# Moving the first weight loads of a fused attention and feed-forward kernel to ScalarE's queue, and a load and its statistics behind the spills and packs

## The reference

```python
x = x + layernorm(attn(layernorm(x)))   # 16 heads of 32, rotary positions,
                                        # each token sees itself and the 128 before it
x = x + layernorm(ffn(layernorm(x)))

def ternary_quant(w):
    scale = mean(abs(w)) + 1e-8
    return clip(round(w / scale), -1, 1) * scale

def ffn(x):                             # W_up, W_gate: 2048 x 512, W_down: 512 x 2048
    up, gate = x @ ternary_quant(W_up).T, x @ ternary_quant(W_gate).T
    return (silu(up) * gate) @ ternary_quant(W_down).T
```

## Time and profile before

| what | value |
|---|---|
| median of 3 runs | 1320.64 us (1318.81 to 1321.5) |
| the profiled execution | 1321.27 us, its span 1319.1 us |
| granted TensorE clock, mean | 0.994 |
| TensorE busy | 1289.1 us (98% of the span) |
| VectorE busy | 938.5 us (71%) |
| ScalarE busy | 794.9 us (60%) |
| GpSimd busy | 709.1 us (54%) |
| DMA | 178.17 MB, mean 135 GB/s |

### The profile page before, as it was taken

The page is one execution under the profiler, slowest core; times in us unless marked ns, Lnnn a source line. Parts: engine busy times, 40 slices in busy tenths (PEclk is TensorE's granted clock), DMA queues, the critical chain, the costliest instruction groups (busy, mean ns, idle before and its releaser), DMA issues.

```text
span 1319.1 us, 28382 instructions
## 1 busy us (share of the span) xinstructions
PE 1289.1 (98%) x9972; PEld 909.3 (69%) x9972; DVE 938.5 (71%) x2421; ACT 794.9 (60%) x1468; POOL 709.1 (54%) x959
## 2 busy tenths in 40 slices
PE   8889999999999999999999999999999999999997
PEld 6566766767677766767677676777667677666775
DVE  7777888776788767876778777787678767634333
ACT  3798887666465665656665665656656556533332
POOL 3365778645655546645565465555566353425432
PEclk9899999999999999999999999999999999999999
DMA  7865657757677577775688576876767746610000
GB/s 233 257 183 161 179 144 145 162 111 155 137 156 162 117 157 150 165 143 120 131 164 171 120 151 134 160 161 120 153 118 170 144 87 123 126 33 25 25 17 33
DMA packets 392797, 178.17 MB, mean 135 GB/s; under 512 B 318416, under 2 KB 372048, under 8 KB 392656
## 3 DMA queue, kind: packets, MB, share of 16 engines
q1 hardware_dynamic: 391792, 174.79, 60.5%
q10 hardware_dynamic: 864, 1.57, 0.4%
HBM read 71.89 MB, written 25.17 MB: 74 GB/s over the span
## 4 chain that ended last, share of the span: by engine, by line
PE 90%; DVE 3%; DMA 2%; ACT 2%; issue 1%; POOL 0%; SPq 0%; ACTq 0%; POOLq 0%; DVEq 0%
PE J L1613 29%; PE Y L1631 16%; PE J L1550 14%; PE J L1541 8%; PE J L1560 8%; PE S L1613 5%; PE O L1525 4%; PE S L1493 3%; PE Y L1501 1%; DMA W<-in_w_qkv 1%; DMA Qp<-spill 1%; DMA spill<-split 1%; PE S L1489 1%; PE S L1490 1%; DVE room L1324 0%
## 5 line engine op out<-in xcount | busy, mean ns | idle before, releaser
L1631 PE MATMUL Y<-down_q,room 128*128 128x512 fp8e4 x1024 | 262.3, 379 | 0.6 <-DVE room L1340 0.6
L1550 PE MATMUL J<-xnT,W 128*128 128x512 f32 x512 | 242.7, 600 | 2.5 <-ACT xnT L977 2.4
L1018 ACT ACTIVATE prob<-prob,peak 128x256 f32<-128x256 f32 x512 | 229.7, 498 | 16.9 <-DVE peak L1270 16.7
L1270 DVE CUSTOM_DVE_ANT_0 prob<-S,band,neg_score_scale 128x256 f32<-128x256 f32 x512 | 225.7, 478 | 10.4 <-PE S L1490 5.4
L1613 PE MATMUL J<-xT,gate_q 128*128 128x256 f16 x1760 | 210.2, 273 | 4.1 <-DVE room L1324 4.1
L1613 PE MATMUL J<-xT,up_q 128*128 128x256 f16 x1776 | 212.0, 273 | 0.0
L1074 ACT ACTIVATE room<-J,sig_scale 128x512 f32<-128x512 f32 x111 | 76.2, 687 | 215.1 <-PE J L1613 215.1
L1613 PEld LDWEIGHTS J<-xT,gate_q 128*128 128x128 fp8e4 x1760 | 171.3, 98 | 49.5 <-DVE room L1324 8.7
L1613 PEld LDWEIGHTS J<-xT,up_q 128*128 128x128 fp8e4 x1776 | 173.4, 98 | 43.8 <-DVE room L1334 1.6
L1324 DVE SCALAR_TENSOR_TENSOR room<-room,J 128x512 f32<-128x512 f32 x111 | 76.3, 687 | 173.8 <-ACT room L1074 173.8
L868 POOL TENSOR_TENSOR o_n<-o_raw,rinv 128x128 f32<-128x128 f32 x128 | 53.9, 421 | 270.3 <-DVE rinv L1299 270.0
(11 more groups left out here) (171 smaller groups left out, 2020.6 us busy)
## 6 DMA issues: line engine op xcount, KB each, us to landing
spill<-split SPq DMA_DIRECT2D x64, 256.0 KB, 2.5
Qp<-spill SPq DMA_DIRECT2D x127, 128.0 KB, 2.9
Kp<-spill SPq DMA_DIRECT2D x125, 128.0 KB, 2.9
x_in<-in_x SPq DMA_DIRECT2D x32, 256.0 KB, 3.2
X<-in_x SPq DMA_DIRECT2D x32, 256.0 KB, 3.4
out_x<-X SPq DMA_DIRECT2D x32, 256.0 KB, 3.2
Kc<-Kp SPq DMA_DIRECT2D x32, 128.0 KB, 3.0
turned<-parts SPq DMA_TRANSPOSE x198, 3.2
```

Of the source, the lines that this page charges most:

```text
L1018: e = nc.scalar.activation(prob[:, prob_home(U), a, :], prob[:, prob_home(U), a, :], ACT.Exp, bias=peak[:, prob_home(U), a:a + 1], scale=-1.0)
L1270: e = nc.vector.tensor_tensor_reduce(out=prob[:, prob_home(U), a, :], in0=S_ps[U % 2][:, a * 2 * P:(a + 1) * 2 * P], in1=mask[:], scale=ne ...
L1550: e = pe.matmul(dst[:], W[:, part, c, g * P:(g + 1) * P], xnT[:, c, :], start=(c == 0), stop=(c == DC - 1))
L1631: e = pe.matmul(Y_ps[t][:], h[:, q % HELD, part, (a * HT + t) * P:(a * HT + t + 1) * P], down_q[:, 2 * pair + a, :], start=(pair == 0 and ...
```

## The change

Raw pieces 2 and 3 are issued by ScalarE ahead of slot 0, behind a wait for the packed K of group 0; pieces 4 to 7 by ScalarE in slots 0 to 3, ahead of the slot's sum. SP issues, ahead of slot 0, the spills of Q and K of group 1, then their packs, and then x of tile 1. VectorE takes the statistics of the four blocks of that x in slots 6, 7, 9 and 9 and the moments in slot 9; GpSimd computes rstd in slot 10. Later tiles keep their slots.

```diff
-LOAD_AT = [-1, -1, -1, -1, -1, -1, -1, 3,
+LOAD_AT = [-1, -1, -1, -1, 0, 1, 2, 3,
...
+FIRST_X_STATS, X_STATS = [6, 7, 9, 9], [4, 5, 6, 7]
...
             pack_k_row(sp, 0, 0)
-            sp.wait_ge(k_packed, 64)
-            for m in (2, 3):
-                load_raw(sp, m)
             spill_q(0, 1)
-            load_raw(sp, 4)
+            spill_k(0, 1)
+            pack_q(0, 1)
+            pack_k(0, 1)
             for t in range(TT):
                 load_x(1, t)
-            load_raw(sp, 5)
-            spill_k(0, 1)
-            load_raw(sp, 6)
-            pack_q(0, 1)
-            pack_k(0, 1)
...
-                for m in range(3 * PIECES):
+                for m in range(PIECES, 3 * PIECES):
                     if s == LOAD_AT[m]:
                         load_raw(sp, m)
...
-                if u == 9 and i + 1 < NM:
+                if u == (9 if i else 10) and i + 1 < NM:
                     rstd_of_x(i + 1)
...
             rotated_high(("Q", 1, 0))
+            act.wait_ge(k_packed, 64)
+            for m in (2, 3):
+                load_raw(act, m)
             exp(0)
...
                 if s == 0:
                     rotated_high(("K", 1, 0))
+                for m in range(PIECES):
+                    if s == LOAD_AT[m]:
+                        load_raw(act, m)
...
                 if i + 1 < NM:
-                    if 4 <= u < 4 + TT:
-                        layer_norm_stats(i + 1, u - 4)
-                    if u == 8:
+                    for t in range(TT):
+                        if u == (X_STATS if i else FIRST_X_STATS)[t]:
+                            layer_norm_stats(i + 1, t)
+                    if u == (8 if i else 9):
                         layer_norm_moments(i + 1)
```

## The result

| kernel | median | runs | profiled execution, its span |
|---|---|---|---|
| before | 1320.58 us (1318.81 to 1322.66) | 16 | 1321.27 us, 1319.1 us |
| changed | 1323.68 us (1321.97 to 1328.83) | 16 | 1328.83 us, 1326.7 us |

The changed kernel is 3.1 us slower, ratio 1.0025 [1.0019, 1.0031]. I had predicted 2.0 us faster, and the time is outside my range (1316.0 to 1322.2).

A forecast was written before the change was run, and what follows sets the result against it. TensorE was taken to bound the kernel (90% of the chain), stalling 3.07 us before unit 8 for the packs. 5.6 - 0.2 - 0.3 - 1.2 - 1.87 = 2.0 us gained: median 1318.6 us, range 1316.0 to 1322.2.

The forecast's parts named there:

- Part 1: TensorE's 3.07 us stall before unit 8 in slot 6 goes, as packs land earlier: gain 5.6 us at slot 8.
- my own cover of 1.8 us: Pack K lands near 47.7, 1.8 us before TensorE asks for it at 49.46; by the skill's rule 0.5 us of stall stays.
- Part 2: ScalarE's six DMA issues cost 0.2 us, and the Q spill sharing the DMA engines with raw 2 costs 0.3 us.
- Rival 3: ScalarE pays full price for issues and the late raw 2 (1.35 + 0.6): gain 0.55 us, 1320.1 us; chance 0.10.
- Part 3: Two of x's statistics move to slot 9, where VectorE has almost no gap: 1.2 us lost.
- Part 4: GpSimd's rstd of x moves from slot 9 to 10, delaying rot of K3 and xnT: 1.87 us lost.
- Rival 1: GpSimd's delay from rstd in slot 10 is hidden: gain 3.9 us, 1316.8 us; chance 0.25.
- Rival 2: K packs land no earlier beside raw pieces on a second queue: 3.1 us slower, 1323.7 us; chance 0.13.

The follow-up runs named there:

- e6: The changed kernel with raw pieces 5 to 7 issued by SP at about 9 us, behind the masks: 1317.73 us, 0.9974 of the kernel before.
- the square: Four kernels on one chip (s1 to s4): raw pieces in two queues or one, rstd behind slot 10's sine product or ahead; 1323.48, 1320.6, 1321.24, 1318.75 us.
- e9: The changed kernel with all raw pieces in SP's one queue, the same transfers ahead of the K pack: 1321.2 us, 0.9998 of the kernel before.
- s3: As e9, on the chip of the square (one queue, rstd behind the product): 1321.24 us, 0.9999 of the kernel before.
- s4: e9 with rstd ahead of slot 10's sine product, on the chip of the square: 1318.75 us, 0.9981 of the kernel before.
- e3: The kernel before with only pieces 2 to 7 moved to ScalarE's queue; x ahead of the K spill, old statistics and rstd slots: 1321.78 us, 1.0008.
- e2: The kernel before with only rstd of x of tile 1 moved from slot 9 to slot 10: 1321.42 us, 1.0006.
- e5: The changed kernel with rstd ahead of slot 10's sine product instead of behind it: 1320.57 us, 0.9998 of the kernel before.
- e1: The kernel before with only the change's slots for statistics, moments and rstd of x of tile 1, all DMAs as they were: 1322.85 us, 1.0022.
- a2: The changed kernel once more, unaltered, for a second profile: 1323.47 us, 1.0023 of the kernel before.
- s1: The changed kernel, unaltered, on the chip of the square (two queues, rstd behind the product): 1323.48 us, 1.0019 of the kernel before.
- s2: As e5, on the chip of the square (two queues, rstd ahead of the product): 1320.6 us, 0.9999 of the kernel before.

## Why the prediction was wrong

**What bounds it: right.** Unit 8's wait for the packs, and half clock behind it. e6 took the wait away, the total of W_up came 5.1 us earlier, and the median followed by 3.4 us with the costs of parts 3 and 4 still in it.

**Part 1: the step that failed.** It read "I let the spill land near 41.5, pack K go out at 41.5 to 43.2 and land near 47.7". Measured in the changed kernel: the spill was issued at 38.39 and landed at 44.5, pack K went out at 44.53 and landed near 54.6, where TensorE restarts. Three things were wrong in it. First, I served the queues in the order of their issues at 403 GB/s, as if they were one. From 41 us on they run side by side, and the whole moves less (283 GB/s from 38 to 42 us). The spill takes 5.7 to 7.5 us so and 4.9 to 5.1 in one queue, and the square puts the price at 2.2 and 1.9 us. Second, my prices were too low even for one queue: there the spill takes 5 us where I gave it 3.3, so the pack goes out at 43.14 to 43.37 (e9, s3, s4), and its rows take 5.8 to 6.1 us where I gave about 4.5. Third, I left piece 7 out of what is ahead of the pack of K: it goes out in slot 3 at 42.11, 2.4 us before the pack. Of the wait, 1.5 to 2.1 us are left in one queue.

I had weighed the rule of the Trainium skill (DMA: Bandwidth & Descriptors, Issuing engines are not separate DMA queues), by which a second queue saves only the time of issuing, and took my own cover of 1.8 us instead. e3 agrees with it: 399 GB/s in two queues, and a wait of 3.65 us. The profiles of the change lie below it: 283 to 336 GB/s, where one queue moved 401 to 406. Why SP's spill hardly moved for its first 2.5 us, and why the engines ran at 127 to 260 GB/s from 40 to 41, stays open.

**Part 2: right, and smaller than priced.** 0.2 + 0.3 us forecast. The issues hide behind running activations, ScalarE has no gap from 38.9 to 53 us, and its wait for raw 2 is 0.75 instead of 0.68 us. Rival 3 is out: its 1.35 us of issues would have to be gaps on ScalarE, and there are none.

**Part 3: mechanism right, size nearly.** 1.2 us forecast, 1.0 measured (total to swap).

**Part 4: mechanism right.** 1.87 us forecast. GpSimd's four instructions take 1.86 us (74.55 to 76.41), and ScalarE's split comes 1.6 us later, all of which reaches xnT. Of the 0.25 us between, 0.35 come back at the addition to rot, which starts 1.41 us behind the product where it started 1.76 us behind it before (with a wait of 0.49), and 0.1 is lost before the four instructions start. Rival 1, hiding, is out: split to xnT is 17.15 to 17.17 us in every row. In the medians the same edit is worth 2.9 and 2.5 us in the square's pairs, and by the ratio 0.8 +- 1.2 in e2. All three intervals hold the 1.6 us of the timeline, so no run shows that the pairs' extra 1 us is real; e5 against the change (about 3 us, on different chips) hints at it, and it stays open.

**Rival 2: what happened, with luck in the number.** It asked for a pack of K landing at 51.5 or later, because raw pieces "take turns with the spill and the packs on the same full DMA engines". The pack landed near 54.6 in this profile. The engines were shared but not full: 85% from 38 to 42 us. The rival put the costs left at 1.2 + 1.87 = 3.1 us; e1, which has just these, measured 2.9 +- 1.4 us (1.0022), and the change 3.1. By the timelines these costs are 1.0 + 1.6 = 2.6 us, and the total of W_up, which the rival took as unmoved, came from 1.4 us earlier to 1.7 us later in the three profiles of the change (0.5 us later in the mean). That the sum is 1323.7 to 0.1 us is luck; that the gain was eaten is not. I gave it 0.13 although its evidence stood in my own rows: the spill of 7.4 us in full engines. "1 MB of x is certainly out of the way" was true, and in one queue it brings the pack of K out 2.3 to 2.5 us earlier (43.14 to 43.37 against 45.66). In two queues half or more of that is lost again (44.45 to 45.76).

## What to carry to other kernels

In this kernel, with busy DMA engines, moving bulk loads to another engine's queue did not take them out of the way of an urgent transfer: it took away the order by which the urgent one came before the later pieces. What worked here was to keep bulk loads behind the urgent ones in the same queue, or to start them in a stretch where the DMA engines are idle (from 18 us on, 0.45% faster). And work moved by one slot "into slack" is priced where it arrives: two statistics and four small instructions cost 2.6 us by the timelines, in slots whose engines had no gap. Last, one profile of such a kernel is one draw: read a wait that depends on DMA in two or three executions before it is priced.

## What the runs showed of the hardware

- With spill and packs in one queue and weight pieces in another, the DMA engines moved 283, 335, 336, 283 and 311 GB/s from 38 to 42 us (changed, a2, s1, e5, s2). With the same transfers in one queue they moved 402, 406 and 401 (e9, s3, s4). With x ahead of the spill in the first queue, two queues moved 399 (e3). So it is not the number of queues alone; the property that decides was not tried.
- In those five profiles the spill, 256 KB issued at 38.2 to 38.7, had moved next to nothing by 41 us (0 to 22 packets on its queue from 39 to 41). From 42 to 43 its queue had 50 to 65% of the engines' time.
- With two queues the wait before unit 8 varied from 2.39 to 6.91 us between executions of kernels that are alike up to there; with one queue from 1.46 to 2.10.
- The six matmuls at xnT took 2.81 us at a granted clock of 1.00 (a2) and 4.51 at about half of it (before, 0.51 from 96 to 98 us), after the same wait of 2.02 us; in profiles of one kernel (the change) 2.81 and 4.09 both occur. From xnT to the end of the span that is 1222.3 against 1224.0 us, so a single profile can be 1.7 us off by this alone.
